# Attention with a feed-forward block: P times V in four 32-column tiles, denominators from sums on GpSimd

## The chip, the cores and the metric

The kernel runs on one core of a Trainium2 chip. The metric is device time in microseconds (us) of one execution; a time quoted for a kernel is the median of its runs. Five engines work side by side and meet only at semaphores: PE (TensorE, the matmuls), DVE (VectorE), ACT (ScalarE), POOL (GpSimd) and SP (SyncE, which here issues most DMAs). PE's weight loads are listed apart, as PEld.

## The reference

```python
x  = L0_attn_x                        # (8, 1024, 512), float32
xn = layernorm(x)                     # over the last axis, eps 1e-5
# attention: 16 heads of 32 columns, causal
q, k, v = split(xn @ W_attn + b_attn, 3)          # heads to the front
att = softmax(where(causal, q @ k.T * 32**-0.5, -inf))
y   = (att @ v) @ W_proj + b_proj
# feed-forward in blockwise FP4 (16 columns to a block), width 1408
h   = silu(fp4(xn) @ fp4(w_gate).T) * (fp4(xn) @ fp4(w_up).T)
out = x + y + fp4(h) @ fp4(w_down).T
```

Both biases are random with a spread of 0.1.

## The kernel before

`attention` runs first, over 8 batches (the span's first 57%), then `feed_forward`; the change lies in `attention` alone. A batch is worked in three stages: a dense stage (projections to q, k and v, `split_product`, L675), the pairs (eight pairs of heads, one after another) and the output stage (`output`, L787, with the next batch's first transposes).

**The pairs.** Scores are needed twice. `scores` (L686) makes them with queries on the partitions, 16 tiles of 128 to 1024 columns for a pair, only to take row maxima on DVE (`row_max`, L470); two PSUM banks take turns, a large tile in `ps_s` and a small one in bank 0 of `ps_dense`. PE turns the finished maxima round (`maxima`, L707), DVE splits them (`split_max`, L477), and a DMA puts them into the operands of the pair after. `transposed_scores` (L711) makes the scores again with keys on the partitions and the maxima taken off, into a ring of three PSUM banks (`ST_RING`). ACT takes exp of each piece into `pt` (L628), and `times_v` (L727) multiplies that by V.

The list `UNITS` (L57) sets the order: 12 units for a pair, first the query half c=1 with key tiles 0 to 7, then c=0 with key tiles 0 to 3. A unit has one piece of up to 512 columns for each of the two heads, so two pieces. In a unit PE's order is `transposed_scores`, one tile of the next pair's (or, late in a pair, the one after it) `scores`, `times_v` of the unit before (`LAG`), and where `SHARE` (L65) gives the unit two tiles, the second. The unit in which `maxima` stands, `M_UNIT`, has no score tile.

**P times V.** In `times_v` each head takes 64 of PE's columns: its 32 columns of V and 32 columns of ones next to them (`v_ones`, L201), so that 32 rows of the result are y and 32 are the softmax denominator. The product is float32 by float32, for which the trace has two MATMULs each. Both heads of a unit write one PSUM bank, side by side in its partitions (`y_rows`, L206):

```python
last = nc.tensor.matmul(y_bank(n)[row:row + HP, off:QC], v_ones(kt, p, h),
                        pt[:, w % PT_RING, h, 0:QC - off], start=kt == 0,
                        stop=kt == (c + 1) * PER - 1)
```

**Division.** DVE copies a finished bank to SBUF (`leave`, L485). SP sends the denominator rows to a compact tile, DVE takes reciprocals (`invert`, L503), SP sends them out and broadcasts them back (`invert` at L328), and POOL multiplies (L419). For the last pair the reciprocal is taken on a whole bank (`invert_last`, L492).

**Output stage.** After the last `times_v` PE transposes four tiles of the next batch's x, then makes eight output tiles of four groups each (L790). DVE adds x and bias to each (`add`, L507); POOL has made their sum (`x_and_bias`, L400) from a tile that ACT's queue loads (`load`, L614).

## Time and profile before

| | |
|---|---|
| median of 3 runs | 4201.06 us (4198.33 to 4204.25) |
| the profiled execution's span, first to last instruction | 4203.1 us |
| batches begin | every 300.4 us, eight of them, 2403 us |
| PE busy over the span | 94% |
| DVE, ACT, POOL busy over the span | 61%, 29%, 11% |

The profiled execution is one of its own; its span lies 2 us above the median of the runs. A timeline row gives start and duration in us, the engine, the line of the kernel, the operation, what it writes and reads, and how many instructions it merges; `[idle before <-releaser]` is the time that the engine stood idle before and what ended it. In rows of groups the two numbers after the count are the busy time in us and the mean duration in ns. Matmuls overlap, so what a matmul costs PE is read from its start to the start of the next.

### The profile page before, as it was taken

What the parts mean: (1) busy time and instruction counts of PE and PEld (TensorE: products, weight loads), DVE (VectorE), ACT (ScalarE), POOL (GpSimd) and SP (SyncE); (2) the same over time, 40 slices, a digit from 0 to 9 for tenths busy, and PEclk for the clock granted to TensorE, in tenths of its full rate; (3) what the DMA queues carried; (4) which work ended last, traced back from release to release, by engine and by line L of the source; (5) the groups of instructions that cost most, each with busy time, mean ns of one, the idle gap of its engine ahead of it and who ended that gap; (6) DMA issues with size and microseconds to landing.
All of it is one profiled execution on the core that took longest, in us unless ns stands there. A gap on an engine that the chain in (4) does not pass through costs nothing. (4 is left out here: it accounts for less than half of the span.)

```text
span 4203.1 us, 57729 instructions
## 1 busy us (share of the span) xinstructions
PE 3970.2 (94%) x19140; PEld 2709.8 (64%) x19140; DVE 2556.4 (61%) x3630; ACT 1198.7 (29%) x2295; POOL 467.1 (11%) x464
## 2 busy tenths in 40 slices
PE   6999999999999999999999943999999999999998
PEld 5546546546556555555565423888888888888887
DVE  4554554544544545545545477777777777777776
ACT  1341431432432422423413412222222222222221
POOL 1121121130130220120221210000000000000000
PEclk9999999999999999999999966999999999999999
DMA  4414425324325225234235121011011100110010
GB/s 150 113 41 161 93 59 160 80 67 147 73 87 144 58 94 140 53 119 128 53 122 126 31 81 48 25 35 32 30 30 35 32 30 30 35 32 30 30 35 28
DMA packets 157523, 304.35 MB, mean 72 GB/s; under 512 B 39296, under 2 KB 41344, under 8 KB 157312
## 3 DMA queue, kind: packets, MB, share of 16 engines
q1 hardware_dynamic: 138880, 268.14, 23.0%
q10 hardware_dynamic: 18432, 33.56, 2.4%
q8 instruction: 112, 1.84, 0.2%
q14 instruction: 99, 0.81, 0.1%
HBM read 196.87 MB, written 101.13 MB: 71 GB/s over the span
## 5 line engine op out<-in xcount | busy, mean ns | idle before, releaser
L1185 PE MATMUL f_ps<-wgu,xqt 128*128 128x512 f32 (+1 forms) x4608 | 992.9, 373 | 17.4 <-DVE h L1040 14.5
L1185 PEld LDWEIGHTS f_ps<-wgu,xqt 128*128 128x128 f32 x4608 | 841.4, 188 | 153.9 <-DVE h L1040 29.9
L628 ACT ACTIVATE pt<-ps_st 128x512 f32<-128x512 f32 (+3 forms) x1536 | 671.6, 488 | 881.0 <-PE ps_st L724 549.4
L474 DVE TENSOR_REDUCE mx<-ps_s 128x1 f32<-128x640 f32 (+3 forms) x576 | 554.7, 963 | 403.3 <-PE ps_s L704 401.5
L1195 PE MATMUL f_ps_o<-wd,hqt 128*128 128x512 f32 x2112 | 512.6, 395 | 2.2 <-DVE hqt L1047 2.2
L738 PE MATMUL ps_dense<-pt,v 128*64 128x512 f32 (+3 forms) x2048 | 472.3, 540 | 0.1
L419 POOL TENSOR_TENSOR yt<-ysum,stage 32x512 f32<-32x512 f32 x256 | 324.7, 1269 | 1211.0 <-DMA stage<-inv_scratch 1120.2
L1195 PEld LDWEIGHTS f_ps_o<-wd,hqt 128*128 128x128 f32 x2112 | 392.6, 189 | 81.0 <-DVE hqt L1047 2.6
L681 PE MATMUL ps_dense<-arena,wa 128*128 128x512 f32 x1536 | 407.9, 412 | 8.9 <-DVE ob L515 7.5
L681 PEld LDWEIGHTS ps_dense<-arena,wa 128*128 128x128 f32 x1536 | 289.2, 195 | 75.6 <-issue 11.7
L474 DVE TENSOR_REDUCE mx<-ps_dense 128x1 f32<-128x512 f32 x448 | 218.8, 488 | 170.7 <-PE ps_dense L704 164.4
L612 ACT ACTIVATE stage<-ps_dense,bqk 128x512 fp32r<-128x512 f32 x128 | 88.1, 688 | 652.7 <-PE ps_dense L681 652.7
L720 PE MATMUL ps_st<-stack 98*128 98x512 f32 (+3 forms) x768 | 267.0, 414 | 0.0
L720 PE MATMUL ps_st<-arena 98*128 98x512 f32 (+3 forms) x768 | 266.9, 414 | 0.0
L724 PE MATMUL ps_st<-identb,causal 128*128 128x128 bf16 x1024 | 231.3, 231 | 0.0
L720 PEld LDWEIGHTS ps_st<-arena 98*128 98x128 f32 x768 | 140.5, 197 | 135.7 <-ACT pt L628 104.6
L790 PE MATMUL ps_dense<-wp,yt 128*128 128x512 f32 x512 | 224.9, 596 | 2.4 <-DVE ob L515 2.3
L1115 ACT ACTIVATE silu<-f_ps 128x512 f32<-128x512 f32 (+1 forms) x192 | 107.0, 557 | 373.8 <-PE f_ps L1185 373.8
L702 PE MATMUL ps_s<-stack 96*128 96x512 f32 (+1 forms) x576 | 176.0, 378 | 35.0 <-DMA stack<-ones_scratch 20.9
L720 PEld LDWEIGHTS ps_st<-stack 98*128 98x128 f32 x768 | 142.7, 201 | 99.5 <-ACT pt L628 66.7
L681 PE MATMUL ps_dense<-wa,arena 128*128 128x512 f32 x768 | 194.0, 401 | 0.0
L738 PE MATMUL ps_y<-pt,v 128*64 128x512 f32 (+3 forms) x1024 | 192.6, 457 | 0.0
(100 smaller groups left out, 4177.9 us busy)
## 6 DMA issues: line engine op xcount, KB each, us to landing
qk_scratch<-stage SPq DMA_DIRECT2D x128, 512.0 KB, 3.0
stack<-qk_scratch SPq DMA_DIRECT2D x192, 256.0 KB
arena<-qk_scratch SPq DMA_DIRECT2D x192, 256.0 KB
xs<-in_L_attn_x SPq DMA_DIRECT2D x64, 256.0 KB, 3.7
res<-in_L_attn_x ACTq DMA_DIRECT2D x64, 256.0 KB, 3.4
acc_scratch<-ob ACTq DMA_DIRECT2D x64, 256.0 KB, 2.2
xt<-in_L_attn_x SPq DMA_DIRECT2D x64, 256.0 KB, 2.6
at<-acc_scratch SPq DMA_DIRECT2D x64, 256.0 KB, 2.6
```

The lines of the kernel that those rows point to most:

```text
L419: nc.gpsimd.tensor_tensor(yt[rows, p * 2 // HG, cols], ysum[rows, n], over_heads()[rows, cols].bitcast(F32), ALU.mult).then_inc(y_div, 1)
L474: nc.vector.tensor_reduce(mx[:, h * ST + q:h * ST + q + 1], scores_bank(p, n)[:, 0:(q + 1) * P], axis=AX.X, op=ALU.max, negate=True).then_ ...
L628: nc.scalar.activation(pt[:, w % PT_RING, h, 0:QC - off], ps_st[:, (2 * w + h) % ST_RING, 0:QC - off], ACT.Exp, scale=SCALE).then_inc(st_e ...
L681: last = nc.tensor.matmul(bank(*use), left(lh, k), right(rh, k), start=n == 0, stop=n == len(terms) - 1)
L702: last = nc.tensor.matmul(out[:, k0:k1], qs, stack(p)[0:KS, 2 + h, k0:k1], start=True, stop=k1 < keys)
L720: last = nc.tensor.matmul(out, stack(p)[0:KM, 2 + h, kt * P:(kt + 1) * P], stack(p)[0:KM, h, c * QC + off:(c + 1) * QC], start=True, stop= ...
L724: last = nc.tensor.matmul(out[:, 0:P], causal[:, :], identb[:, :], start=False, stop=True)
L738: last = nc.tensor.matmul(y_bank(n)[row:row + HP, off:QC], v_ones(kt, p, h), pt[:, w % PT_RING, h, 0:QC - off], start=kt == 0, stop=kt == ...
L790: last = nc.tensor.matmul(bank("P", k), yt[:, g, t * P:(t + 1) * P], wp[:, g, :], start=g == 0, stop=g == G - 1)
L1115: nc.scalar.activation(silu[:, c, 0:n], ps[:, [0, 1, 1][c], 0, 0:n], ACT.Silu).then_inc(s_done, 1)
L1185: last = nc.tensor.matmul(ps[:, [0, 1, 1][c], gu, 0:n], xqt[:, a, k], wgu[:, b, gu, k, f:f + n], start=i == 0, stop=i == len(terms) - 1)
L1195: last = nc.tensor.matmul(ps_o[:, :], hqt[:, a, k], wd[:, b, k], start=i == 0, stop=i == len(terms) - 1)
```

## The change

- **Order by key tile.** `UNITS` goes. A pair has 8 units, one for each key tile, and `PARTS` lists a unit's pieces for both query halves: four pieces for key tiles 0 to 3, two for 4 to 7. The number of pieces, 24 for a pair, and their widths stay. The ring of three banks stays. Each unit has two score tiles, also the one with `maxima`, which is now unit 3.
- **P times V.** Each head's query tiles are split by parity, and the four combinations take 32 of PE's columns each, without ones. A PSUM bank holds a whole pair's y. `pt` keeps all the queries of a key tile; key tiles 5 to 7 go to a buffer that shares memory with the output stage (`rob`).
- **Denominators.** POOL adds the exponentials of key tiles 0 to 4 into `stage` (`sum_up`; in the last pair 0 to 2). In unit 1 of the next pair PE multiplies those sums and the remaining key tiles by 32 columns of ones (`denominators`); in the last pair right after `times_v`.
- **Division** moves from POOL to DVE (`divide`), in unit 7 of the next pair and, for the last two pairs, after the pair loop. `leave` goes; DVE copies a bank of denominators in its place (`copy_den`).
- **v's bias** is no longer added to v: once, ahead of the batches, it is multiplied by W_proj and added to the output bias.
- In the output stage the first two tiles' residuals are loaded after the last denominators rather than ahead of the pairs, and the fourth transposition follows the first parts of two outputs.

```diff
-    UNITS = [(c, kt, max(0, kt * P - c * QC)) for c in reversed(range(NQ)) for kt in range((c + 1) * PER)]
-    NU = len(UNITS)
-    ENDS = [i + 1 for i, (c, kt, _) in enumerate(UNITS) if kt == (c + 1) * PER - 1]
+
+    PARTS = [[(h, max(c * QC, kt * P), (c + 1) * QC - max(c * QC, kt * P))
+              for c in reversed(range(NQ)) if (c + 1) * QC > kt * P for h in range(2)] for kt in range(ST)]
+    NPARTS = sum(len(parts) for parts in PARTS)
+    PART0 = [sum(len(parts) for parts in PARTS[:kt]) for kt in range(ST + 1)]
     ST_RING, PT_RING, SLOTS, XR = 3, 3, 4, 4
 
+    RINGED = 5
+    TAIL0 = {kt: 2 * P * sum(ST - k for k in range(RINGED, kt)) for kt in range(RINGED, ST)}
+    TAIL = 2 * P * sum(ST - k for k in range(RINGED, ST))
+
+    def summed(p):
+
+        return RINGED if p < PAIRS - 1 else 3
+
+    SUMS = sum(summed(p) for p in range(PAIRS))
...
-    SHARE = [2 if off == 0 else 1 if off < QC - P else 0 for _, _, off in UNITS]
-    M_UNIT = ENDS[0] - 1
-    EARLY = sum(SHARE[M_UNIT + 1:])
+    SHARE = TILES // ST
+    M_UNIT = ST // 2 - 1
+    EARLY = TILES - SHARE * (M_UNIT + 1)
     LAG = 1
-    INV_UNIT = LAG + 2
-    assert sum(SHARE) == TILES and SHARE[M_UNIT] == 0
+    DEN_UNIT = 1
+    Y_UNIT = ST - 1
...
+        def parity_tiles(kt, s):
+            return kt + (s - kt) % 2
+        def y_rows(h, s):
+            first = (h + 2 * s) * HD
+            return slice(first, first + HD)
+        def y_cols(kt, s):
+            return slice(parity_tiles(kt, s) // 2 * P, QC)
...
 # GpSimd
+                def sum_up(p, kt):
+
+                    pool.wait_ge(st_exp, ONE + b * PAIRS * NPARTS + p * NPARTS + PART0[kt + 1])
+                    if kt > 1:
+                        pool.wait_ge(summed_up, ONE + b * SUMS + p * RINGED + kt)
+                    cols = slice(kt * P, S)
+                    both = stage[:, :, :, :].rearrange("p h a n -> p h (a n)")
+                    ring = lambda k: pt[:, (p * RINGED + k) % PT_RING]
+                    if kt == 0:
+                        nc.gpsimd.tensor_tensor(both[:, :, 0:P], ring(0)[:, :, 0:P], ones[:, 0:1].unsqueeze(2).to_broadcast([P, 2, P]),
+                                                ALU.mult).then_inc(summed_up, 1)
+                    else:
+                        nc.gpsimd.tensor_tensor(both[:, :, cols], (ring(0) if kt == 1 else both)[:, :, cols], ring(kt)[:, :, cols],
+                                                ALU.add).then_inc(summed_up, 1)
...
+                    for kt in range(summed(p)):
+                        if kt == 0 and p:
+                            pool.wait_ge(den_full, ONE + b * PAIRS + p)
+                        sum_up(p, kt)
...
 # VectorE, in the pair loop
+                        if u == DEN_UNIT and p:
+                            copy_den(p - 1)
+                        for n in tiles:
                             row_max(*n)
                         if u == M_UNIT and p + 1 < PAIRS:
                             split_max(p + 1)
-                        if u == INV_UNIT and p:
+                        if u == M_UNIT and p:
                             invert(p - 1)
+                        if u == Y_UNIT and p and p < PAIRS - 1:
+                            divide(p - 1)
+                invert_last()
+                divide(PAIRS - 2)
+                divide(PAIRS - 1)
...
 # ScalarE
+                        before = p * RINGED + kt - PT_RING
+                        if kt < RINGED and before >= 0:
+                            pp, pk = divmod(before, RINGED)
+                            act.wait_ge(pv_done, ONE + b * PAIRS * ST + pp * ST + pk + 1)
+                            act.wait_ge(summed_up, ONE + b * SUMS + pp * RINGED + max(pk, 1) + 1)
...
 # TensorE
+                def transposed_scores(p, kt):
+
+                    for i, (h, q, n) in enumerate(PARTS[kt]):
+                        w = p * NPARTS + PART0[kt] + i
+
+                        pe.wait_ge(st_exp, ONE + b * PAIRS * NPARTS + max(w - ST_RING + 1, 0))
+                        out = ps_st[:, w % ST_RING, 0:n]
+                        diagonal = q == kt * P
                         last = nc.tensor.matmul(out, stack(p)[0:KM, 2 + h, kt * P:(kt + 1) * P],
-                                                stack(p)[0:KM, h, c * QC + off:(c + 1) * QC], start=True,
-                                                stop=not diagonal)
+                                                stack(p)[0:KM, h, q:q + n], start=True, stop=not diagonal)
...
+                def times_v(p, kt):
+
+                    if kt == 0 and p > 1:
+                        pe.wait_ge(y_div, ONE + b * PAIRS * 2 + (p - 1) * 2)
+                    pe.wait_ge(st_exp, ONE + b * PAIRS * NPARTS + p * NPARTS + PART0[kt + 1])
+                    for s in range(2):
+                        if parity_tiles(kt, s) >= ST:
+                            continue
+                        for h in range(2):
+                            last = nc.tensor.matmul(by_tile(y_bank(p)[y_rows(h, s), y_cols(kt, s)]), v_head(kt, p, h),
+                                                    exps_of_parity(p, kt, h, s), start=kt == 0, stop=kt == ST - 2 + s)
                     last.then_inc(pv_done, 1)
+
+                def denominators(p):
+                    pe.wait_ge(summed_up, ONE + b * SUMS + p * RINGED + summed(p))
+                    if p + 2 < PAIRS:
+                        pe.wait_ge(s_max, ONE + b * PAIRS * TILES + (p + 2) * TILES + EARLY + SHARE * DEN_UNIT)
+                    for kt in range(summed(p) - 1, ST):
+                        for s in range(2):
+                            if parity_tiles(kt, s) >= ST:
+                                continue
+                            for h in range(2):
+                                if kt < summed(p):
+                                    src, cols = by_tile(sums(h))[:, s::2], slice(0, QC)
+                                else:
+                                    src, cols = exps_of_parity(p, kt, h, s), y_cols(kt, s)
+                                last = nc.tensor.matmul(by_tile(den_bank(p)[y_rows(h, s), cols]), ones[:, :], src,
+                                                        start=kt < summed(p), stop=kt == ST - 2 + s)
+                    last.then_inc(den_full, 1)
...
                     transposed_scores(p, u)
+                    if u == DEN_UNIT and p:
+                        denominators(p - 1)
                     if u == M_UNIT and p + 1 < PAIRS:
                         maxima(p + 1)
+                denominators(PAIRS - 1)
```

What the change does to PE's order in a unit: here are the rows of unit 1 (key tile 1, query half 1) of a middle pair before. L720 is `transposed_scores`, L702 and L704 a score tile and its mask, L738 `times_v`; REGISTER_ALU rows compute what a wait compares with.

```order
L720 MATMUL ps_st<-stack 128x512
L717 REGISTER_ALU
L720 MATMUL ps_st<-stack 128x512
L697 REGISTER_ALU
L702 MATMUL ps_s<-arena 128x512
L702 MATMUL ps_s<-arena 128x128
L704 MATMUL ps_s<-causal,identb 128x128
L735 REGISTER_ALU
L738 MATMUL ps_dense<-pt,v 64x512 x2
L697 REGISTER_ALU
L702 MATMUL ps_dense<-arena 128x512
L704 MATMUL ps_dense<-causal,identb 128x128
```

And of unit 1 of a pair in the changed kernel, from its third piece to the end of the denominators (L763 and L766 are the transposed scores and their mask, L795 the denominators):

```order
L763 MATMUL ps_st<-stack 128x384
L766 MATMUL ps_st<-identb,causal 128x128
L760 REGISTER_ALU
L763 MATMUL ps_st<-stack 128x384
L766 MATMUL ps_st<-identb,causal 128x128
L783 ISA
L785 REGISTER_ALU
L795 MATMUL ps_dense<-stage,ones 32x512 x4
L795 MATMUL ps_dense<-rob,ones 32x128 x2
L795 MATMUL ps_dense<-rob,ones 32x256 x2
L795 MATMUL ps_dense<-rob,ones 32x128 x6
L741 REGISTER_ALU
```

Two more pieces stand ahead of the rows shown, so four follow each other with no other work between; each has its own wait for a free bank of the ring.

Where the maxima are turned round on PE, before:

```order
L738 MATMUL ps_dense<-pt,v 64x384 x2
L720 MATMUL ps_st<-stack 128x128
L724 MATMUL ps_st<-identb,causal 128x128
L717 REGISTER_ALU
L720 MATMUL ps_st<-stack 128x128
L724 MATMUL ps_st<-identb,causal 128x128
L735 REGISTER_ALU
L738 MATMUL ps_dense<-pt,v 64x256 x2
L708 REGISTER_ALU
L709 MATMUL ps_dense<-ident,mx 128x128
```

and now (L746 and L748 are the score tiles, L778 `times_v`, L753 is the transposition of the maxima):

```order
L746 MATMUL ps_s<-arena 128x512 x2
L748 MATMUL ps_s<-causal,identb 128x128
L778 MATMUL ps_y<-pt,v 32x384 x4
L741 REGISTER_ALU
L746 MATMUL ps_dense<-arena 128x128
L748 MATMUL ps_dense<-causal,identb 128x128
L752 REGISTER_ALU
L753 MATMUL ps_dense<-ident,mx 128x128
```

The last two score tiles, whose maxima the transposition reads, stood a unit ahead of it and now stand in the same unit.

## Rows read from the trace of the kernel before

**Rows 1.** The page: the span, and each engine's busy time.
```profile
span 4203.1 us, 57729 instructions
PE 3970.2 (94%) x19140; PEld 2709.8 (64%) x19140; DVE 2556.4 (61%) x3630; ACT 1198.7 (29%) x2295; POOL 467.1 (11%) x464
```

**Rows 2.** Stretches: a middle pair, the last pair, the output stage; columns in the first row.
```profile
core 0: us, PE busy (x) PEld busy (x) DVE busy (x) ACT busy (x) POOL busy (x), PEclk, DMA share, GB/s
473.74:497.74 24.00, 24.00 (x132) 12.20 (x130) 13.86 (x21) 10.51 (x24) 5.06 (x4) 1.00 0.35 80
592.14:610.10 17.96, 17.96 (x94) 7.65 (x92) 9.75 (x20) 10.46 (x24) 8.47 (x12) 1.00 0.14 44
610.10:642.10 32.00, 30.12 (x82) 13.53 (x80) 12.06 (x14) 2.17 (x4) 12.64 (x10) 1.00 0.46 149
```

**Rows 3.** Timeline of PE in a unit of 512 columns.
```profile
572.84 1.08 PE L738 MATMUL ps_dense<-pt,v 128*64 128x512 f32 x4
573.85 0.33 PE L702 MATMUL ps_dense<-arena 96*128 96x128 f32 x1
574.01 0.23 PE L704 MATMUL ps_dense<-causal,identb 128*128 128x128 bf16 x1
574.05 0.71 PE L720 MATMUL ps_st<-arena 98*128 98x512 f32 x2
574.60 0.39 PE L702 MATMUL ps_s<-arena 96*128 96x512 f32 x1
```

**Rows 4.** Line L738 within that unit: count, ns min/median/max, first and last start.
```profile
L738 PEld LDWEIGHTS ps_dense<-pt,v x4: 133/134/136, 572.8 to 572.9; 128*64 128x64 f32 x4
L738 PE MATMUL ps_dense<-pt,v x4: 592/618/643, 572.8 to 573.3; 128*64 128x512 f32 x4
```

**Rows 5.** Timeline of PE around the end of a diagonal unit.
```profile
562.64 0.47 PE L720 MATMUL ps_st<-stack 98*128 98x512 f32 x1
...
563.00 0.48 PE L720 MATMUL ps_st<-stack 98*128 98x512 f32 x1
...
563.36 0.53 PE L702 MATMUL ps_s<-arena 96*128 96x512 f32 x2
563.74 0.23 PE L704 MATMUL ps_s<-causal,identb 128*128 128x128 bf16 x1
563.90 0.44 PE L738 MATMUL ps_dense<-pt,v 128*64 128x128 f32 x4
564.27 0.50 PE L702 MATMUL ps_dense<-arena 96*128 96x512 f32 x1
```

**Rows 6.** From a piece to its exponentials: a PE row and an ACT row.
```profile
592.14 0.73 PE L720 MATMUL ps_st<-arena 98*128 98x512 f32 x2
592.68 2.12 ACT L628 ACTIVATE pt<-ps_st 128x512 f32<-128x512 f32 x4 [0.73 <-PE ps_st L720]
```

**Rows 7.** Timeline of DVE, the largest and the smallest row maximum.
```profile
572.94 1.22 DVE L474 TENSOR_REDUCE mx<-ps_s 128x1 f32<-128x1024 f32 x1
574.28 0.29 DVE L474 TENSOR_REDUCE mx<-ps_dense 128x1 f32<-128x128 f32 x1
```

**Rows 8.** Groups on POOL: sums of 512 columns and of one.
```profile
L402 POOL TENSOR_TENSOR res<-res,bp 128x512 f32<-128x512 f32 x64 | 81.0, 1271 | 583.6 <-DMA res<-in_L_attn_x 583.6
L389 POOL TENSOR_TENSOR mv<-mv,eps 128x1 f32<-128x1 f32 x64 | 13.9, 217 | 175.1 <-DVE mv L449 175.1
```

**Rows 9.** Timeline of PE in the output stage, with the next batch's first product.
```profile
612.75 10.66 PE L790 MATMUL ps_dense<-wp,yt 128*128 128x512 f32 x24
623.70 17.43 PE L790 MATMUL ps_dense<-wp,yt 128*128 128x512 f32 x40 [0.30 <-DVE ob L515]
642.11 0.73 PE L681 MATMUL ps_dense<-arena,wa 128*128 128x512 f32 x2 [0.98 <-DVE ob L515]
```

**Rows 10.** DVE: the reciprocal of a bank (group), and an add (timeline).
```profile
L501 DVE RECIPROCAL ob<-ps_dense 128x512 f32<-128x512 f32 x8 | 26.9, 3358 | 42.5 <-PE ps_dense L738 42.5
622.95 0.69 DVE L515 TENSOR_TENSOR ob<-ps_dense,res 128x512 f32<-128x512 f32 x1 [3.31 <-POOL yt L419]
```

More of the change, by code:

```diff
@@ L344, in body @@
                 for p in range(PAIRS):
                     if p:
-                        invert(p - 1)
+                        den_rows(p - 1)
                     if p + 1 < PAIRS:
                         maxima(p + 1)
+                    if p:
+                        spread(p - 1)
+                    if p == PAIRS - 3 and not final:
+                        for t in range(XR):
+                            load_x(b + 1, t)
                     if p + SLOTS < PAIRS:
-                        sp.wait_ge(st_exp, ONE + b * PAIRS * NU * 2 + (p + 1) * NU * 2)
+                        sp.wait_ge(st_exp, ONE + b * PAIRS * NPARTS + (p + 1) * NPARTS)
@@ L375, in _ @@
             pool.memset(mhalf[:, :], -0.5)
-            pool.memset(v[:, :], 1.0).then_inc(consts, 1)
+            pool.memset(ones[:, :], 1.0).then_inc(consts, 1)
             pool.wait_ge(zeroed, 1)
@@ new lines, in body @@
+                for i in range(2):
+                    pool.wait_ge(qk_out[i], ONE + b * (NQK // 2) * DMA + (NQK // 2) * DMA)
+                for p in range(PAIRS):
+                    if p == PAIRS - 1 and not final:
+                        inv_std(b + 1, 0, XR)
+                    for kt in range(summed(p)):
+                        if kt == 0 and p:
+                            pool.wait_ge(den_full, ONE + b * PAIRS + p)
+                        sum_up(p, kt)
+                pool.wait_ge(bias_sum, 1)
@@ L429, in body @@
+                for t in range(ST):
                     x_and_bias(t)
@@ L438, in _ @@
                 nc.vector.tensor_tensor(wa[:, 1, k], w_stage(k), wa[:, 0, k].bitcast(F32), ALU.subtract).then_inc(w_lo, 1)
-            dve.wait_ge(b_load, 5 * DMA)
+            dve.wait_ge(b_load, 4 * DMA)
             dve.wait_ge(consts, 2)
+            for k in range(KC):
+                nc.vector.tensor_scalar(yt[:, k, 0:P], ident[:, :], 0.0, bvc[:, k:k + 1], ALU.mult, ALU.add).then_inc(bias_cols, 1)
             def stats(b, t):
@@ L552, in body @@
                 for p in range(PAIRS):
[L553 removed]
+                    for u in range(ST):
                         tiles = beside(p, u)
[L555 to L563 removed]
+                        if u == DEN_UNIT and p:
+                            copy_den(p - 1)
+                        for n in tiles:
                             row_max(*n)
@@ L647, in _ @@
             pe.wait_ge(w_lo, KC)
-            pe.wait_ge(b_load, 5 * DMA)
+            pe.wait_ge(b_load, 4 * DMA)
             pe.wait_ge(consts, 2)
+            for k in range(KC):
+                pe.wait_ge(bias_cols, k + 1)
+                last = nc.tensor.matmul(ps_y[:, :], yt[:, k, 0:P], wp[:, k, :], start=k == 0, stop=k == KC - 1)
+            last.then_inc(bias_full, 1)
             def transpose_x(b, t):
@@ L725, in transposed_scores @@
                         last.then_inc(st_full, 1)
-                def times_v(p, u):
-                    c, kt, off = UNITS[u]
-                    n = 0 if u < ENDS[0] else 1
-                    if kt == 0:
-                        pe.wait_ge(y_copy, ONE + b * PAIRS * NQ + max(p * NQ + n - 1, 0))
-                    w = p * NU + u
-                    pe.wait_ge(st_exp, ONE + b * PAIRS * NU * 2 + 2 * w + 2)
-                    for h in range(2):
-                        row = y_rows(p, h)[0]
-                        last = nc.tensor.matmul(y_bank(n)[row:row + HP, off:QC], v_ones(kt, p, h),
-                                                pt[:, w % PT_RING, h, 0:QC - off], start=kt == 0,
-                                                stop=kt == (c + 1) * PER - 1)
-                    last.then_inc(pv_done, 1)
+                def times_v(p, kt):
[8 more added lines that the diff above has]
+                                                    exps_of_parity(p, kt, h, s), start=kt == 0, stop=kt == ST - 2 + s)
+                    last.then_inc(pv_done, 1)
@@ L764, in body @@
                     scores(1, n)
-                for w in range(PAIRS * NU):
-                    p, u = divmod(w, NU)
+                for w in range(PAIRS * ST):
+                    p, u = divmod(w, ST)
                     tiles = beside(p, u)
```

275 lines of the change are left out of this document (129 added, 146 removed).

## The prediction

> **What bounds the kernel now.** I read the page first: PE is busy for 94% of the span, the next engine for 61% [rows 1]. Then the stretches: a middle pair takes 24.00 us and PE is busy for all of it, DVE for 13.9, ACT for 10.5, POOL for 5.1; the last pair takes 17.96 us, again all PE's; the output stage takes 32.0 us with 30.1 of PE work [rows 2]. The granted clock is 1.00 (of 2.4 GHz) in all three. So PE's order of instructions is the path, and a microsecond taken from PE counts in full as long as nobody makes it wait. What others wait for on PE costs nothing today; what PE waits for after the change costs in full. Last the timelines, for what a piece of work costs PE, start to start.
>
> **P times V before.** A 512-column group of both heads runs from 572.84 to 573.85, 1.01 us [rows 3]; one of 128 columns from 563.90 to 564.27, 0.37 [rows 5]; so 0.213 for each 128 columns, and 0.80 and 0.58 for 384 and 256 (by interpolation). Other matmuls start 0.04 after a mask (574.01 to 574.05), L738 0.16 after it (563.74 to 563.90) [rows 3, 5]: 0.12 to enter a group. A pair has six groups of 512 and two of each other width: 6.06 + 1.60 + 1.16 + 0.74 + 12 x 0.12 = **11.0 us**. Both heads run at once: the four MATMULs start between 572.8 and 573.3 and last some 0.62 each, two by two [rows 4].
>
> **P times V after.** The widest parity of key tiles 0 to 7 has 512, 512, 384, 384, 256, 256, 128, 128 columns. If four tiles run at once as two do, that is 2 x (1.01 + 0.80 + 0.58 + 0.37) + 8 x 0.12 + 0.1 for sixteen more starts = **6.6 us**. The denominators are one entry and four groups behind each other, 512, 256, 128, 128 columns. Without the way in and out a group is two passes of 0.427, 0.213 or 0.107 and about 0.05 after each: 0.96 + 0.53 + 0.32 + 0.32, with entry and exit **2.35 us**. Together 2.05 us less than before.
>
> **The ring of three.** Before, a unit had two pieces for three banks. Now key tiles 0 to 3 have four, and the fourth waits until exp of the first is done. From a first piece to its exp are 0.54 us (592.14 to 592.68), and four exps take 2.12, so one takes 0.59 where three follow every 0.51 [rows 6]. PE starts again some 0.05 after a release (the add ends at 623.64, the matmul starts at 623.70) [rows 9, 10]. The fourth piece so starts 1.19 us after the first, where PE would get to it at about 0.85. It and its mask take 0.36 [rows 5], 0.055 less for each 128 columns fewer: 1.12 for the four widths. Four units: 4 x 1.19 + 1.12 = 5.88. Before, the same pieces cost 4 x 0.55 (574.05 to 574.60) [rows 3] and 0.72 (562.64 to 563.36) [rows 5], 0.61, 0.50, 0.40: 4.43. That is **+1.45 us**. Then the score tile behind a four-piece unit follows a mask, not a long matmul, and its weights are exposed for about 0.08: **+0.3**. Bounds for the two: 0.7, if PE had been waiting at such places anyway or the release comes sooner, to 2.6, if the fourth piece's weights (0.19 a load, of which the row hides all) are loaded only after the wait.
>
> **The maxima.** They turned round a unit after the last score tile; now both tiles of unit 3 stand right ahead. From the start of the large tile: 0.55 to its mask, 0.23 + 0.03 to DVE, 1.22 for the maximum of 1024 columns and 0.29 for that of 128 [rows 7], 0.05 back: 2.4. PE has meanwhile the tile (0.55), 0.16, `times_v` of 384 columns (0.80) and the small tile (0.2), 1.7. With its weights exposed too: **+0.75 us**, in seven pairs of eight. Bounds 0.4 to 1.0.
>
> **GpSimd.** From 512 columns in 1.271 and one in 0.217 [rows 8] come 0.217 + 2.06 ns a column, for a pair's 5888 columns 13.2 us of 24: hidden. The one that ACT waits for is key tile 1's, 1792 columns, 3.9 us. It starts when the denominators are done and key tile 0's copy is made. Unit 0 is 1.55 for its pieces, 0.54 and 0.38 for its score tiles and 0.37 for `times_v`, 2.8; unit 1 has 1.5 of pieces and the denominators, 6.7; the copy of 256 columns (0.75) and hand-overs give 7.7 us into a pair, so the sum ends at 11.6. Unit 1 ends at 8.6 (two tiles and `times_v`, 1.9), unit 2 3.4 later, and exp of key tile 3 wants the sum 0.54 after that, at 12.6. One microsecond of slack; in the last pair, which has no scores, 0.4 is missing. Copy, reciprocal and division on DVE add some 2 us where 1.35 for `leave` goes: 15 of 24 us, hidden; the division's factors come 6 us after the reciprocal at the latest and are wanted at the pair's end. SP's new waits stand ahead of loads for a pair three further on. v's bias, the residual's later load and the smaller memset lie behind the first x or beside PE's eight outputs: nothing.
>
> The Trainium skill (TensorE: Matmul & The Clock Gate, Part 3, The mechanism) has weight loads overlap matmuls in flight only where the row group differs; column tiles share their rows. Here the second pass's loads start within 0.1 us of the first pass's start [rows 4], so the trace disagrees, and I take them as hidden.
>
> **Output stage.** After the last `times_v` come the denominators of the last pair, with key tiles 3 to 7 not summed: 0.96 + 0.75 + 2 x 0.53 + 2 x 0.32 + 0.2 = 3.6 us. Then DVE's reciprocal, 3.36, and two products of 0.69 [rows 10]: 8.5 us, before which the second output can't start. Its six matmuls of 0.43 (64 of them fill the rows from 612.75 to 641.1) [rows 9], a transposition (0.5) and four more bring 13.4; DVE's last `low_of_x` and the first add end at 14.2; 48 matmuls take 20.6 and the next batch's product starts 1.1 later: 36.0 against 32.0. **+4.0 us** a batch; bounds 2 to 7, since the residual's chain can be late once more.
>
> **Sum.** A full pair: -2.05 + 1.45 + 0.3 + 0.75 = +0.45. A batch: the first pair has no denominators before it, -1.9; six pairs, +2.7; the last has neither maxima nor scores, -0.2 with POOL's delay; output stage +4.0 (the denominators are in it). **+4.6 us a batch, +37 in all**; the feed-forward block is untouched. The profiled execution's 4203.1 becomes 4240, and against the median of 4201.06, 2 us below it, about **4236 us**: what is taken from P times V is given back in waits on ACT and DVE that the old order didn't have.
>
> **The rivals.**
> *The waits are smaller, and it gains.* For it: PE's busy time has modelled ends, and if the fourth pieces and the turn of the maxima wait at their lower bounds, a full pair gains 2.05 - 0.7 - 0.4 = 0.95 us. Seven such pairs and 2.9 for the first, less 2 to 4 in the output stage, give about 5 a batch: 4160. Against it: the ring has three banks for four pieces whatever else happens. Chance 0.20.
> *The four tiles don't run four at once.* The trace has only two at once [rows 4]. If they run two by two, P times V of a pair is 10.6 us and the denominators 3.9, +5.6 a pair: 4236 + 64 x 5.6 = about 4600; if a third is lost, 4236 + 64 x 8.95 / 3 = about 4430. The Trainium skill (TensorE: Matmul & The Clock Gate, Part 3, Measured speedup vs the span model) has three column tiles at 2.38 times one, somewhat less than three. The rule on weight loads would belong here too: 88 loads of 0.134 a pair, +11.8, would give 4990, and I hold it for one in a hundred. For the whole 0.11.
> *GpSimd is too slow.* Its rows are of one block of columns; the new ones have two and are up to 3.5 times as long. The sum of key tile 1 decides from 2.6 ns a column; at 3.1 it is 0.9 us late in each pair, 4290; from some 4 ns POOL itself is the bound. It stops nobody today [rows 2]. Chance 0.09.
> The forecast as told has 0.60.
>
> **How the numbers follow.** A measurement can tell about 0.2%, 8 us, from no change. Within the forecast +37 has an uncertainty of some 25 (half a microsecond a pair is 32): of its 0.60 I give 0.05 to faster, 0.08 to the same and 0.47 to slower. The first rival gives 0.17 to faster and 0.03 to the same, the others 0.20 to slower: 0.22, 0.11, 0.67. The forecast's own range is 4195 to 4275; it must reach down to the first rival and up to a late GpSimd, and leaves the tiles out: **4160 to 4300**.
>
> **What would show it.** Right: middle pairs of 24.2 to 24.7 us; `times_v` groups of eight MATMULs in 1.01 us at 512 columns; idle PE of 0.3 us at the fourth piece, released by ACT, in units 0 to 3 and 0.7 ahead of the transposition, by DVE; an output stage of 36 us. Wrong: pairs under 23.5; eight MATMULs in two groups of four; exps released by POOL.

## The result and the profile after

| | before | after |
|---|---|---|
| median (lowest to highest), us | 4202.66 (4198.33 to 4205.38), 4 runs | 4230.41 (4228.15 to 4232.83), 4 runs |
| span of the profiled execution, us | 4203.1 | 4231.0 |
| batches follow each other, mean distance, us | 301.1 | 303.7 |

The changed kernel is slower: ratio 1.0067, 95% interval 1.0052 to 1.0081. The forecast was 4236 us, with a chance of 0.67 for slower. (The 300.4 us from batch to batch given for the kernel before is the usual distance; the mean is 301.1, since two batches took 2.6 us more.) The page of after, against [rows 1]:

```profile
span 4231.0 us, 63428 instructions
PE 3907.3 (92%) x21836; PEld 2737.0 (65%) x21836; DVE 2586.1 (61%) x3683; ACT 1172.8 (28%) x2295; POOL 926.7 (22%) x464
```

PE is busy for 63 us less and the span is 28 us longer: PE stands idle 91 us more. Stretches of after, against [rows 2]: the first pair of the second batch, a middle pair, the last pair, the output stage (to the next batch's first product); columns in the first row.

```profile
core 0: us, PE busy (x) PEld busy (x) DVE busy (x) ACT busy (x) POOL busy (x), PEclk, DMA share, GB/s
429.50:454.30 24.80, 24.07 (x139) 13.03 (x139) 12.69 (x19) 10.28 (x24) 13.33 (x5) 0.79 0.37 78
501.49:525.07 23.58, 22.23 (x172) 12.07 (x171) 14.45 (x23) 10.06 (x24) 13.32 (x5) 1.00 0.35 82
592.59:610.10 17.51, 15.77 (x138) 7.83 (x138) 7.22 (x8) 10.05 (x25) 9.13 (x4) 1.00 0.12 30
610.10:644.98 34.88, 32.95 (x128) 15.60 (x125) 13.89 (x17) 2.17 (x4) 10.08 (x8) 1.00 0.46 144
```

A middle pair got **0.41 us shorter**, where +0.45 was forecast; the first has a mean granted clock of 0.79. The second batch, stretch by stretch, from the starts of PE's rows:

| stretch | before | after | difference | forecast |
|---|---|---|---|---|
| first score tile to first pair | 36.88 | 41.26 | +4.38 | 0 |
| pair 0 | 24.35 | 24.80 | +0.45 | -1.9 |
| pairs 1 to 5 | 119.94 | 117.92 | -2.02 | +2.25 |
| pair 6 | 22.45 | 20.38 | -2.07 | +0.45 |
| last pair | 17.96 | 17.51 | -0.45 | -0.2 |
| output stage | 32.00 | 34.88 | +2.88 | +4.0 |
| projections up to the next first score tile | 46.77 | 46.27 | -0.50 | 0 |
| sum | 300.35 | 303.02 | **+2.67** | +4.6 |

Inside a middle pair: PE's timeline of units 0 and 1 (L763 and L766 are the transposed scores, L746 and L748 a score tile, L778 `times_v`, L795 the denominators), with the first `times_v` of 512 columns behind them.

```profile
501.46 0.94 PE L763 MATMUL ps_st<-arena 98*128 98x512 f32 x3
502.24 0.23 PE L766 MATMUL ps_st<-identb,causal 128*128 128x128 bf16 x1
502.62 0.50 PE L763 MATMUL ps_st<-arena 98*128 98x512 f32 x1
502.96 0.23 PE L766 MATMUL ps_st<-identb,causal 128*128 128x128 bf16 x1
503.01 0.54 PE L746 MATMUL ps_s<-stack 96*128 96x512 f32 x2
...
505.88 1.06 PE L795 MATMUL ps_dense<-stage,ones 128*32 128x512 f32 x8
506.77 1.05 PE L795 MATMUL ps_dense<-rob,ones 128*32 128x128 f32 x20
507.75 0.62 PE L746 MATMUL ps_s<-stack 96*128 96x512 f32 x2
508.21 0.23 PE L748 MATMUL ps_s<-causal,identb 128*128 128x128 bf16 x1
508.37 1.07 PE L778 MATMUL ps_y<-pt,v 128*32 128x512 f32 x8
509.37 0.44 PE L746 MATMUL ps_dense<-stack 96*128 96x384 f32 x1
```

Three things are to be seen. The fourth piece of unit 0 starts at 502.62, 0.38 after the mask before it (502.24), where a row without a wait starts 0.04 after one; in units 1 to 3 it is 0.44, 0.50 and 0.56. Eight MATMULs of `times_v` take 508.37 to 509.37, 1.00 us, where four of them took 1.01 [rows 3]: all four tiles run at once, two MATMULs for each. And the denominators' 28 MATMULs are done in 1.87 us (505.88 to 507.75). The turn of the maxima (L753), at the end of unit 3 of the same pair:

```profile
515.92 0.33 PE L746 MATMUL ps_dense<-stack 96*128 96x128 f32 x1
516.08 0.23 PE L748 MATMUL ps_dense<-causal,identb 128*128 128x128 bf16 x1
516.72 0.33 PE L753 MATMUL ps_dense<-ident,mx 128*128 128x128 f32 x1 [0.40 <-DVE mx L504]
```

It starts 0.64 after the mask, so 0.60 is a wait on DVE. GpSimd and ACT in that pair: the sum of key tile 1 (L440), and the exponentials of key tile 3, which must wait for it.

```profile
507.99 0.61 POOL L437 TENSOR_TENSOR stage<-pt,ones 128x256 f32<-128x256 f32 x1 [10.04 <-PE ps_dense L795]
508.56 4.01 POOL L440 TENSOR_TENSOR stage<-pt 128x1792 f32<-128x1792 f32 x1
...
513.56 1.43 ACT L664 ACTIVATE pt<-ps_st 128x512 f32<-128x512 f32 x4 [1.71 <-PE ps_st L763]
```

The sum is done 11.1 us into the pair and wanted at 12.1: 1.0 us of slack, and PE, not POOL, released ACT. Last, PE's timeline where the +4.38 lies, between the last projection and the first pair:

```profile
422.58 0.59 PE L746 MATMUL ps_s<-stack 96*128 96x512 f32 x2 [0.78 <-DVE v L561]
...
424.15 0.62 PE L746 MATMUL ps_s<-stack 96*128 96x512 f32 x2 [0.56 <-DVE mx L504]
...
425.90 0.82 PE L746 MATMUL ps_s<-stack 96*128 96x512 f32 x2 [0.63 <-DVE mx L504]
...
428.04 1.22 PE L746 MATMUL ps_s<-stack 96*128 96x512 f32 x2 [0.73 <-DVE mx L504]
...
429.50 1.63 PE L763 MATMUL ps_st<-stack 98*128 98x512 f32 x3
```

`EARLY`, the number of score tiles ahead of the pairs, is 8 where it was 4. There is nothing else for PE to do there, so it runs at DVE's pace and waits three times for `mx` where it waited once. Four score tiles have only moved here from beside pair 6: of pair 6's -2.07, about -1.65 is their going (the rest is the -0.41 of any middle pair), so some 2.7 of the 4.38 are a loss. From 426.3, behind the waits that end at 422.58, 424.15 and 425.90, the granted clock is 0.5 for 13.7 us, and the two matmuls of the tile of 1024 columns (428.04) take 1.22 us, where they take 0.71 at full clock (at 514.42). In before the clock fell at this place in two batches of eight, for 6.8 us; in after it falls in all eight, for 10.2 to 17.1 us.

### The profile page after: what moved, and what is told of

The parts are those of the page before. It is cut to its first block and busy times, and to the rows that moved or that the text cites. A ratio compares the mean times of both kernels' runs of the same rounds, so it can differ in the third digit from the quotient of the medians.

```text
span 4231.0 us, 63428 instructions
## 1 busy us (share of the span) xinstructions
PE 3907.3 (92%) x21836; PEld 2737.0 (65%) x21836; DVE 2586.1 (61%) x3683; ACT 1172.8 (28%) x2295; POOL 926.7 (22%) x464
## 5 line engine op out<-in xcount | busy, mean ns | idle before, releaser
L664 ACT ACTIVATE pt<-ps_st 128x512 f32<-128x512 f32 (+3 forms) x1152 | 517.9, 530 | 709.0 <-PE ps_st L763 549.3
L440 POOL TENSOR_TENSOR stage<-stage,pt 128x1536 f32<-128x1536 f32 (+2 forms) x176 | 517.4, 2940 | 26.9 <-ACT pt L664 12.8
L763 PE MATMUL ps_st<-stack 98*128 98x512 f32 (+3 forms) x768 | 264.9, 422 | 27.5 <-ACT pt L664 24.4
L763 PE MATMUL ps_st<-arena 98*128 98x512 f32 (+3 forms) x768 | 252.6, 402 | 37.7 <-ACT pt L664 33.1
L437 POOL TENSOR_TENSOR stage<-pt,ones 128x256 f32<-128x256 f32 x64 | 39.2, 613 | 1125.0 <-ACT pt L664 600.1
L440 POOL TENSOR_TENSOR stage<-pt 128x1792 f32<-128x1792 f32 x64 | 256.4, 4007 | 22.0 <-ACT pt L664 22.0
L766 PE MATMUL ps_st<-identb,causal 128*128 128x128 bf16 x1024 | 238.5, 236 | 0.0
L746 PE MATMUL ps_s<-stack 96*128 96x512 f32 (+1 forms) x576 | 191.6, 407 | 42.1 <-DMA stack<-ones_scratch 20.2
L763 PEld LDWEIGHTS ps_st<-arena 98*128 98x128 f32 x768 | 138.6, 194 | 109.1 <-ACT pt L664 80.0
L1098 DVE TENSOR_TENSOR h<-silu,f_ps 128x512 f32<-128x512 f32 (+1 forms) x192 | 122.4, 637 | 101.1 <-ACT silu L1173 101.1
```

Source lines behind the costliest of these rows:

```text
L440: nc.gpsimd.tensor_tensor(both[:, :, cols], (ring(0) if kt == 1 else both)[:, :, cols], ring(kt)[:, :, cols], ALU.add).then_inc(summed_up, 1)
L664: nc.scalar.activation(a[:, q - first * P:q - first * P + n], ps_st[:, w % ST_RING, 0:n], ACT.Exp, scale=SCALE).then_inc(st_exp, 1)
L746: last = nc.tensor.matmul(out[:, k0:k1], qs, stack(p)[0:KS, 2 + h, k0:k1], start=True, stop=k1 < keys)
L763: last = nc.tensor.matmul(out, stack(p)[0:KM, 2 + h, kt * P:(kt + 1) * P], stack(p)[0:KM, h, q:q + n], start=True, stop=not diagonal)
L766: last = nc.tensor.matmul(out[:, 0:P], causal[:, :], identb[:, :], start=False, stop=True)
L1098: nc.vector.tensor_tensor(h[:, f:f + n], silu[:, c, 0:n], ps[:, [0, 1, 1][c], 1, 0:n], ALU.mult).then_inc(h_mul, 1)
```

## The experiments

Theory: three costs sit on top of a shorter P times V, and each can be taken off alone: the wait for the ring of three (1.4 us a pair), the wait for the maxima (0.6), and idle time with half clock around the eight early tiles (some 4 us a batch). The rival to each: the wait only moves. Each run's ratio is to the kernel before, run on the same chip; the experiments ran on four chips, so times of different runs are compared by their ratios where the difference is small. Where a kernel has fillers, these are matmuls with unused results that take the place of idle time.

**The changed kernel again**, as the base.

> The changed kernel itself, on the same chip as the next three. Every theory: about 28 us over the kernel before (4230 against 4202); middle pairs of 23.58 us.

Measured: 4229.4 us (4228.53 to 4232.16), ratio 1.0066 (1.0052 to 1.0080).

**A score tile between the second and the third piece.**

```diff
-                    transposed_scores(p, u)
-                    if u == DEN_UNIT and p:
-                        denominators(p - 1)
+                    transposed_scores(p, u, slice(0, 2))
                     for n in tiles[:1]:
                         scores(*n)
+                    transposed_scores(p, u, slice(2, 4))
+                    if u == DEN_UNIT and p:
+                        denominators(p - 1)
```

`transposed_scores` also gets an argument for which of its pieces to issue, and in unit 1 the denominators now stand behind the first score tile.

> A unit's first score tile stands between the second and the third piece of the transposed scores, so that the fourth piece is asked for later; nothing else moves. Theory (ring of three): the idle 0.34 + 0.40 + 0.46 + 0.52 = 1.7 us ahead of the fourth pieces goes in the 56 pairs that have score tiles, less some 0.3 for one more switch of operands: about -1.4 x 56 = -80 us against the changed kernel, middle pairs 22.2 us, some 4150 us. Rival (GpSimd's sum of key tile 1 is the limit just behind): its slack is about 1.0 us, so exp of key tile 3 is released by POOL and a pair falls by 0.7 at most: 4190 us. Rival (the idle time is only modelled and costs nothing): no change, 4230 us.

Measured: 4151.38 us (4150.01 to 4154.92), ratio 0.9882 (0.9867 to 0.9897). The window of a middle pair:

```profile
463.07:485.27 22.20, 21.70 (x172) 11.96 (x171) 14.39 (x23) 10.23 (x24) 13.32 (x5) 1.00 0.39 86
```

1.38 us less than 23.58: the ring's wait is gone. In the pair shown PE no longer waits for ACT, and only 0.11 us is new, for DVE ahead of the first score tile; over attention its waits for ACT fall from 57.5 us (179 times) to 12.4 (17 times). ACT works through the same 24 pieces in about the same time (busy 10.23 us, 10.06 in the changed kernel). One reordering of a few lines turns the loss of 28 us into a gain of 50.

**The turn of the maxima a unit later**, behind the first pieces of unit 4.

```diff
+                    if u == M_UNIT + 1 and p + 1 < PAIRS:
+                        maxima(p + 1)
...
-                    if u == M_UNIT and p + 1 < PAIRS:
-                        maxima(p + 1)
```

> The maxima are turned round after the transposed scores of unit 4 instead of at the end of unit 3. Theory (PE waits there for DVE's last two maxima): the 0.6 us of idle time in 56 pairs go, -34 us against the changed kernel, about 4196 us, middle pairs 22.98 us. Rival (DVE is late next, since its split of the maxima and the reciprocal now come later): the wait moves to the next score tiles, less than half of it is won, 4215 us.

Measured: 4188.6 us (4183.08 to 4194.31), ratio 0.9970 (0.9958 to 0.9982); a middle pair takes 22.95, 0.63 less. PE's waits by what it waited for (line waited for: us in total, times, longest), of the changed kernel up to 2420 us (all but the last pair of the last batch) and of this one to the end of attention:

```profile
PE ps_st L763 <- ACT pt L664: 56.1, 177, 1.3
PE ps_dense L753 <- DVE mx L504: 22.6, 56, 0.4
...
PE ps_s L746 <- DVE mx L504: 15.7, 24, 0.9
```

```profile
PE ps_st L763 <- ACT pt L664: 61.3, 203, 1.3
...
PE ps_s L746 <- DVE mx L504: 16.0, 24, 0.9
```

The row of L753 (56 times, seven pairs of eight batches) is gone, and little of it has moved: to the end of attention PE waits 61.3 us for ACT, where the changed kernel waits 57.5. The time fell by more than expected (4188.6 against 4196).

**Two fillers after every second early tile.**

```diff
                 for n in range(EARLY):
                     scores(1, n)
+                    if n % 2 and n < EARLY - 1:
+                        for _ in range(FILL):
+                            nc.tensor.matmul(ps_st[:, 0, :], wa[:, 0, 0, 0:P], wa[:, 0, 0, 0:QC], start=True, stop=True)
```

> Two dummy matmuls of 512 columns (0.43 us, result unused) behind the second, fourth and sixth of the eight score tiles ahead of the pairs, where PE waits for DVE. Theory (the granted clock falls to 0.5 there and the first 10 us of pair 0 run at it): the clock stays 1.00, pair 0 takes 21.6 instead of 24.8 us, -3.2 x 8 = -26 us, about 4205 us. Rival (pair 0 is slow for another reason, a late load or DVE's backlog): nothing changes or it is up to 5 us longer, 4230 to 4235 us.

Measured: 4190.64 us (4183.08 to 4195.32), ratio 0.9965 (0.9951 to 0.9978). The window of the second batch's first pair, where after had 24.80 at 0.79:

```profile
425.06:446.13 21.07, 19.72 (x139) 10.79 (x139) 12.77 (x19) 10.06 (x24) 13.38 (x5) 1.00 0.47 99
```

It is 21.07 or 21.08 in the first seven batches and 21.14 in the last, so the half clock there costs 3.7 us a batch; and the way to the pair is 40.40 instead of 41.26. Work that does nothing made the kernel 39 us faster, where 26 were expected. This also settles what the clock does with the first pair: the idle time ahead of it brings it down, not the new matmuls.

**Four early tiles again, with the maxima turned in unit 5.**

```diff
-    M_UNIT = ST // 2 - 1
+    M_UNIT = 5
+    INV_UNIT = 3
```

(The reciprocal, the statistics and the normalisation keep their units, and SP now issues `spread` ahead of the maxima.)

> The maxima are turned round in unit 5 instead of 3 (so four score tiles stand ahead of the pairs, as before the change, not eight), the reciprocal stays in unit 3 and SP sends it on ahead of the maxima. Theory (the run of eight tiles ahead of the pairs is bound by DVE and brings the half clock): pair 0 loses its half clock (as with the dummies, -39 us), the run itself is 4.4 us shorter a batch of which 1.6 come back in pair 6 (-23 us); against it the maxima have only units 6 and 7, 3.75 us, where they need 3.9 from PE to the landed copy and start 0.6 late, up to 0.3 us a pair (+17 us): 4184 us. Rival (the maxima come late by more than a microsecond a pair, DVE and SP being busy there): 4230 us or more, pairs of 24.5 us.

Measured: 4219.21 us (4216.1 to 4221.31), ratio 1.0044 (1.0028 to 1.0061): 10 us less than the changed kernel, far from the 4184 that was expected. In the second batch the way to the first pair (35.18) and the first pair (21.22) gain 9.7 us, pair 6 gets its four tiles back (23.56, +3.2). The rest went where the maxima now arrive late; the start of that batch's last pair, and PE's row of waits for the maxima, which the changed kernel doesn't have (its maxima have four units for the way, these two):

```profile
585.29 1.06 PE L764 MATMUL ps_st<-arena 98*128 98x512 f32 x3 [1.35 <-DMA arena<-mr]
586.15 0.33 PE L767 MATMUL ps_st<-identb,causal 128*128 128x128 bf16 x1
```

```profile
PE ps_st L764 <- DMA arena<-mr: 12.9, 12, 1.4
```

About as much again is the wait for the last maxima ahead of their turn: 34.6 us in 56 times, where the changed kernel had 22.6. The masks of 0.33 instead of 0.23 show the second half of the price: the granted clock is 0.5 from 586.0, just behind the wait at 585.29, for 6.8 us.

**Both moves.** The score tile between the pieces, and the later turn.

> The split pieces and the later turn of the maxima together. Theory (with the split 0.4 us of wait for the maxima is left in a pair, by its own trace): -0.4 x 56 = -23 us against the split alone, about 4128 us, pairs of 21.8 us. Rival (the gains add in full): 4151 - 41 = 4110 us. Rival (POOL's sum is now the limit): 4145 us, with idle time of PE released by ACT that waited for POOL.

Measured: 4123.55 us (4118.84 to 4125.79), ratio 0.9819 (0.9802 to 0.9835). A middle pair:

```profile
458.70:480.30 21.60, 21.47 (x171) 11.89 (x172) 14.26 (x23) 10.24 (x24) 13.34 (x5) 1.00 0.39 89
```

Middle pairs mostly take 21.57 to 21.60, just 23.58 - 1.38 - 0.63: in a pair the two waits are independent. The time as a whole does not add: it is 13 us above the 4110 that both gains in full would give. At least a part of that is clock: the eight early tiles bring 13.7 us of half clock in each batch here, in the run with the split alone 13.7 in four batches and 10.2 in four.

**Both moves and the fillers.**

> The same and the dummy matmuls ahead of the pairs. Theory (independent places, the gains add): -39 us against the two, 4089 us. Rival (a shorter pair leaves the clock low elsewhere, in the last pair or the output stage): -20 us or less, 4105 us.

Measured: 4084.6 us (4069.45 to 4100.92), ratio 0.9712 (0.9683 to 0.9742). In the profiled execution, the slowest of the four, the first pair takes 19.7 us in four batches and 22.6 in four, where the clock fell again. The four runs follow their mean granted clocks: 4069 (0.978), 4075 (0.976), 4094 (0.971), 4101 (0.970).

**Both moves and four early tiles.**

> Split, later turn and the maxima in unit 5, so their turn is in unit 6. Theory: 4128 - 39 - 23 and then up to 0.7 us a pair of wait for the maxima's copy (+39 us): 4105 us, pairs of 22.4 us. Rival (the copy lands in time): 4066 us.

Measured: 4202.87 us (4170.17 to 4230.41), ratio 0.9993 (0.9967 to 1.0020). Everything that both moves gained is lost, mostly by the mechanism of the run with four early tiles, now with a wait for the maxima in every second pair. The start of a pair, and two middle pairs:

```profile
468.53 1.22 PE L764 MATMUL ps_st<-arena 98*128 98x512 f32 x2 [1.57 <-DMA arena<-mr]
469.55 0.95 PE L747 MATMUL ps_s<-arena 96*128 96x512 f32 x2
```

```profile
468.50:495.00 26.50, 26.13 (x169) 14.30 (x169) 12.87 (x20) 10.60 (x24) 13.32 (x5) 0.81 0.26 62
495.00:517.40 22.40, 21.93 (x170) 11.94 (x169) 14.57 (x23) 10.38 (x24) 13.32 (x5) 1.00 0.37 85
```

Shorter pairs leave the maxima's way less time: PE waits 22 times for `arena<-mr` and 6 times for `stack<-mr`, up to 2.1 us, and one such wait can be enough for 10.2 us of half clock: a pair of 26.5 beside one of 22.4. Half clock of 6.8 us or more stands beside 19 of these 28 waits. It also stands in five of the eight first pairs (25.8 us against 20.0), which have no such wait, only the two short ones for DVE ahead of them (0.78 and 0.56 us) that the kernel before has too: four early tiles don't keep the clock up by themselves. Both my expectations missed; I had taken the chain from the maxima to their DMA as nearly hidden (up to 0.7 us a pair).

**Nine fillers against six.** `FILL = [2, 2, 3, 2]`, the last two right ahead of the first pair.

> The version with both moves and six fillers, with nine of them: a third one in the third gap and two in the fourth, right ahead of the first pair. The fillers write a bank that is written again at once; their results are unused. In its trace the six fillers left 0.41 us idle ahead of the last large tile and 0.60 us inside the first unit, and the granted clock still fell there in four batches of eight (the first pair 22.64 us with the fall, 19.69 without); its four runs lay between 4069 and 4101 us, in the order of their mean clock. Theory (the idle time beside the eight score tiles is what brings the clock down, and the fall is what spreads the runs): no half clock in the first pair of any batch, first pairs of 19.7 to 20.0 us, 4065 to 4075 us and a spread of under 15 us. Rival (the falls come at random, or from other parts of the kernel): first pairs of 22.6 us again in about half the batches, 4085 us with a spread of 30, and nothing gained from three more fillers.

> The version with both moves and six fillers once more, as the other half of this comparison on one chip. Theory: 4070 to 4100 us as before, the runs in the order of their mean clock, and 10 to 25 us above the one with nine fillers. Rival: level with it.

Measured: nine, 4092.51 us (4081.41 to 4095.07), ratio 0.9738 (0.9725 to 0.9752); six (the version with both moves and the fillers once more), 4089.75 us (4080.3 to 4095.22), ratio 0.9734 (0.9721 to 0.9748). The theory is half right: with nine no first pair had half clock in the profiled execution (19.11 to 19.15 us in all eight batches; with six, two of 22.63), but the times are level, and the 4065 to 4075 us expected for nine were missed. Two falls of 2.95 us are too little for this comparison, and the runs still spread; that falls elsewhere do it is a guess, which the next pair of runs tries.

**Six more fillers in the last pair**, where PE waits for the exponentials behind GpSimd's sum.

```diff
+                    if u == M_UNIT and p == PAIRS - 1:
+                        for _ in range(FILL_LAST):
+                            nc.tensor.matmul(ps_s[:, 0:QC], wa[:, 0, 0, 0:P], wa[:, 0, 0, 0:QC], start=True, stop=True)
```

> The version with nine fillers, and six more in the last pair, into a bank of scores that is free there, between the second and the third piece of unit 3, where PE stands idle for 1.28 us behind the sum on GpSimd (results unused). With nine fillers no first pair had half clock, but the gain over six was lost in the noise; its trace still shows the clock fall for 10.2 us from 1709.2, inside a last pair. Theory (what still spreads the runs are falls that begin in the last pair's wait): no half clock in any last pair or the output stage behind it, a spread of under 8 us, and 4075 to 4083 us. Rival (they belong to the output stage and the projections, which the fillers don't touch): falls there as before, level with nine fillers.

> The version with nine fillers once more, as the other half of this comparison. Theory: 4080 to 4096 us, the runs in the order of their mean clock, 5 to 12 us above the one with fifteen. Rival: level.

Measured: fifteen fillers, 4080.8 us (4076.91 to 4082.54), ratio 0.9713 (0.9699 to 0.9726); nine, 4085.21 us (4077.74 to 4099.44), ratio 0.9717 (0.9703 to 0.9730). The second batch's last pair, with nine fillers and with fifteen:

```profile
571.93 0.33 PE L764 MATMUL ps_st<-arena 98*128 98x128 f32 x1 [1.31 <-ACT pt L665]
572.10 0.23 PE L767 MATMUL ps_st<-identb,causal 128*128 128x128 bf16 x1
572.26 0.85 PE L779 MATMUL ps_y<-pt,v 128*32 128x384 f32 x8
573.04 0.78 PE L764 MATMUL ps_st<-arena 98*128 98x512 f32 x1
```

```profile
566.23 0.74 PE L765 MATMUL ps_st<-arena 98*128 98x512 f32 x2
566.81 1.56 PE L838 MATMUL ps_s<-wa 128*128 128x512 f32 x6
568.21 0.23 PE L765 MATMUL ps_st<-arena 98*128 98x128 f32 x1
```

With nine, the clock falls in three of eight last pairs for 10.2 us (here 0.78 for a piece of 0.48); with fifteen in none, and up to the end of attention the profile has no fall longer than 3.4 us behind the first batch's start. The spread of the runs is 5.6 us against 21.7. But this is a likely reading, not a proof: the profile with nine is of its slowest run (4099.4) and the one with fifteen of its fastest (4076.9), the earlier profile with nine has such a fall in only one last pair, and the medians' difference, 4.4 us, is within the intervals. What holds is the level: this version is 121 us below the kernel before (0.9713), and six fillers (0.9712 and 0.9734) and nine (0.9738 and 0.9717) can't be told from it.

## Why the prediction was right

The sign and the size held (4230 against 4236, within 4160 to 4300), but part of that is luck, two errors that cancel: in the second batch the middle pairs, first pair and pair 6 together came out 4.4 us below the forecast (-3.64 against +0.8), and an untold cost of 4.38 ahead of the pairs took it back. Eight times 4.4 is 35 us, more than the whole difference measured. The signs named beforehand were missed too: middle pairs of 23.58 lie below the 24.2 to 24.7 that would have shown the forecast right, and just above the 23.5 that would have shown it wrong. (A slip of 2 us: 4201.06 + 37 is 4238, not 4236.) Term by term:

- **P times V, 11.0 to 6.6.** Right: 1.00, 0.78, 0.57 and 0.35 us for the four widths, with 0.12 to enter each group 6.4. The rival that the tiles don't run four at once is out. The loads of the second pass are hidden with 32 columns as they were with 64 [rows 4]; 88 exposed loads of 0.108 us would make a pair 9.5 us longer than it is. PE's row of weight loads for `times_v` in the middle pair (40 of its 60):

```profile
L778 PEld LDWEIGHTS ps_y<-pt,v x40: 106/108/109, 508.4 to 520.5; 128*32 128x32 f32 x40
```

  That is where the trace and the Trainium skill's rule on row groups (TensorE: Matmul & The Clock Gate, Part 3, The mechanism), which the prediction weighs, differ once more, and the trace decides.
- **Denominators, 2.35.** Mis-sized: 1.87 + 0.12 = 1.99. I put about 0.05 us behind each of the eight passes and 0.2 for entry and exit. The passes alone are 1.71, so what stands behind each is 0.02, and of the 0.2 only the entry, 0.12, is left. So P times V and denominators together gained 2.6 us, not 2.05.
- **The ring of three, +1.45.** Right: units 0 to 3 need 5.85 us for their pieces, forecast 5.88; and undoing it alone gave 1.38. The exposed weights behind a mask (+0.3) are there too: 0.315 for the first product of a tile there, 0.233 before.
- **The maxima, +0.75.** Right, 0.15 too high: 0.60 by the timeline, 0.63 by the experiment.
- Sum of a middle pair: -2.6 + 1.4 + 0.3 + 0.6 = -0.3, measured -0.41, forecast +0.45. The mechanism was right and sizes were off, the denominators most (0.36), then P times V (0.2) and the maxima (0.15); together they turned the sign of a pair. The first rival, that the waits are smaller (0.7 and 0.4), is out: the pair gained because P times V and the denominators are shorter than forecast.
- **GpSimd.** In full pairs right: ready at 11.1 and wanted at 12.1, forecast 11.6 and 12.6. In the last pair 1.28 us late instead of 0.4. The rate was low: 1792 columns take 4.01 us, 2.24 ns each, where the one row of 512 columns [rows 8] and one of a single column gave 2.06. The last pair still became 0.45 shorter.
- **First pair, -1.9.** Failed, as did "no change" ahead of it. This is the step that failed by its mechanism: the forecast looked at each pair's length and not at `EARLY`, which the change raises from 4 to 8 as a consequence of `M_UNIT`; so it missed the DVE-bound stretch (2.7 us net of the tiles that left pair 6), what it does to the clock (3.7 us), and pair 6. Without the half clock the first pair is 21.07, 3.3 us shorter than before, of which 1.9 were forecast.
- **Output stage, +4.0.** +2.9 in the second batch; the denominators of the last pair took 2.9 us instead of 3.6. From the last pair's start to the next batch's first product it is +2.0 to +2.5 in six batches and +7.2 in the third, where the clock falls in the last pair. The chain I named is there, as DVE's timeline shows: reciprocal from 613.20 (3.36 us), products to 619.26. No run takes this cost off, so that it is this chain's is read from the timeline only. In the last batch, where no transpositions stand between, the way from the last pair's start to the feed-forward block grew by 6.7.

```profile
613.20 3.36 DVE L525 RECIPROCAL dn<-ps_s 128x512 f32<-128x512 f32 x1 [5.47 <-PE ps_s L795]
616.47 1.34 DVE L538 TENSOR_TENSOR yt<-ps_dense,rob 64x512 f32<-64x512 f32 x2
617.85 1.41 DVE L538 TENSOR_TENSOR yt<-ps_y,dn 64x512 f32<-64x512 f32 x2
```

The whole: seven batches by +2.6, the last one by +8.9 up to the feed-forward block, 1.5 there, -0.8 ahead of the first: +28. (The middle pairs of the last batch take 23.88 in after, 0.3 more than elsewhere; why stays open.)

## What to carry to other kernels

Faster matmuls bring what the order of the work lets through: here 2.6 us a pair were gained, and 2.3 of them given back where four pieces met a ring of three banks and where the last input of a reduction stood right ahead of its reader. The first went away by moving one tile's work into the gap, the second by reading a unit later, so look at each ring for more requests in a row than it has banks, and for other work of the same engine to put between. And when a constant is derived from another (how many tiles stand ahead of the loop), price that stretch too: here a stretch of PE at DVE's pace cost its idle time and then half clock for up to 17 us of full work behind it.

## What was not expected of the hardware

**Short idle times bring the clock down.** Three waits of 0.78, 0.56 and 0.63 us one soon after the other ahead of the first pair were followed, in all eight batches of the changed kernel, by a granted clock of 0.5 (1.2 of 2.4 GHz) for 10.2 to 17.1 us of otherwise full work, beginning at most 1.1 us from the end of the third. With the first two alone it fell in two batches of eight before, in one with four early tiles, and in five with four early tiles and both moves. A single wait of 1.3 us in the last pair did it in one batch of eight in the changed kernel, and for 10.2 us in three of eight in one profile with nine fillers; of the waits for the maxima one of 1.6 us did it and one of 2.1 did not. So it is not certain each time. The runs of one kernel follow their mean granted clock: with four early tiles and both moves the ten runs go from 4170 at a mean clock of 0.961 to 4230 at 0.948.

**DVE waits for GpSimd on an operation in SBUF.** The normalisation of x has one SBUF operand in and out. In before it took 514 to 547 ns; beside GpSimd's sums its line has a longest of 3684 (the row of after first):

```profile
L481 DVE TENSOR_SCALAR xs<-xs,mv x64: 460/536/3684, 30.6 to 2180.2; 128x512 f32<-128x512 f32 x64
```

```profile
L453 DVE TENSOR_SCALAR xs<-xs,mv x64: 514/539/547, 31.1 to 2162.9; 128x512 f32<-128x512 f32 x64
```

In each of seven batches one normalisation of the four starts 0.12 us behind the start of a sum of 1536 columns and ends 0.3 us behind its end (in the second batch 603.13 to 606.82, the sum 603.01 to 606.53). The Trainium skill (SBUF — State Buffer, Who interferes with whom) has a port pair shared by the two engines, which `tensor_scalar` can take in its two-port modes, and which one engine then holds for a whole instruction while the other stands. That fits; no run here tells it from another cause. The row maxima, which read PSUM, show no such thing: 1.22 us before and 1.23 after for 1024 columns.
